# Feature attention as a ring of eight PSUM banks, a transposed output product in the ternary layer, norms computed further ahead, and splits placed behind the negated maxima

## The reference

```python
# L0x, L1x: 16 heads of 16; products are made from three bf16 parts of each fp32 operand
attn = softmax(einsum('bhqd,bhkd->bhqk', q, k) / sqrt(16)); out = (attn @ v) @ wo.T + bo

# L1f: block_quant rounds to 3 mantissa bits, one exponent for each 32 features
h = gelu(block_quant(x) @ block_quant(w_fc).T + b_fc)          # 256 -> 1024
return block_quant(h) @ block_quant(w_proj).T + b_proj         # 1024 -> 256

# L2x: softmax over the 16 FEATURES of a head, for q and for k
q = softmax(_heads(x @ Wq.T + bq), axis=-1)
k = softmax(_heads(y @ Wk.T + bk), axis=-1);  v = _heads(y @ Wv.T + bv)
D_inv = 1.0 / sum(q * sum(k, axis=-2), axis=-1)
out = q + (q @ einsum('bhnd,bhne->bhde', k, v)) * D_inv
return out @ Wp.T + bp

# L2f: weights rounded to -1, 0, 1 by their mean magnitude
h = relu(x @ quantize(W1).T + b1);  return h @ quantize(W2).T + b2
```

## Time and profile before

| what | us |
|---|---|
| median of 3 runs (lowest to highest) | 4759.7 (4759.58 to 4760.19) |
| the profiled execution: its time | 4758.25 |
| the profiled execution: its span | 4756.4 |
| PE busy | 4330.5 (91%) |
| PE weight load busy | 2408.4 (51%) |
| DVE busy | 3124.3 (66%) |
| ACT busy | 2460.3 (52%) |
| POOL busy | 899.1 (19%) |
| softmax_attentions | 0 to 1812 |
| quantised_ffn | 1812 to 2026 |
| feature_attention | 2026 to 2282 |
| ternary_ffn | 2282 to 2588 |
| the two stages after them | 2588 to 4756.4 |

### The profile page before, as it was taken

How to read it: one execution, slowest core, us unless ns; L and a number is a source line. 1 busy time by engine, 2 the same in 40 slices (tenths; PEclk the granted TensorE clock), 3 DMA queues, 4 the chain that set the end, 5 groups by cost and what they waited for, 6 DMA issues and landing times. The chain is left out here.

```text
span 4756.4 us, 67654 instructions
## 1 busy us (share of the span) xinstructions
PE 4330.5 (91%) x23938; PEld 2408.4 (51%) x23938; DVE 3124.3 (66%) x7497; ACT 2460.3 (52%) x5534; POOL 899.1 (19%) x583
## 2 busy tenths in 40 slices
PE   5999999999999995677576999999999998999998
PEld 2333334443333333455354666666666666555555
DVE  5777777777777775778665667767666766334333
ACT  3666666666666665511232677677767676111111
POOL 2322443533223203511243000000000000000000
PEclk8999999999999997889687999999999999999999
DMA  6445345343444420010200011101101101000001
GB/s 146 76 71 82 65 58 89 54 67 67 67 79 73 72 41 22 1 36 13 90 0 16 27 32 31 30 30 30 35 26 30 35 26 41 33 0 0 0 0 36
DMA packets 182204, 205.16 MB, mean 43 GB/s; under 512 B 43704, under 2 KB 164408, under 8 KB 180256
## 3 DMA queue, kind: packets, MB, share of 16 engines
q1 hardware_dynamic: 181920, 201.45, 21.4%
HBM read 140.64 MB, written 60.78 MB: 42 GB/s over the span
## 5 line engine op out<-in xcount | busy, mean ns | idle before, releaser
L461 DVE TENSOR_REDUCE L0x_maxes<-L0x_ps_max 128x1 f32<-128x512 f32 x1536 | 986.1, 684 | 275.7 <-PE L0x_ps_max L726 271.9
L642 ACT ACTIVATE L0x_probs<-L0x_ps_sc 128x1024 f32<-128x1024 f32 x768 | 778.5, 1026 | 413.6 <-PE L0x_ps_sc L715 407.9
L726 PE MATMUL L0x_ps_max<-L0x_kstack,L0x_qstack 96*128 96x512 bf16 x1536 | 593.9, 387 | 20.6 <-DVE L0x_maxes L461 12.4
L2431 ACT ACTIVATE L3x_pexp<-L3x_ps,L3x_nmax 128x77 f32<-128x77 f32 (+2 forms) x1536 | 600.3, 432 | 0.0
L715 PE MATMUL L0x_ps_sc<-L0x_qstack,L0x_kstack 104*128 104x512 bf16 x1536 | 523.3, 382 | 8.9 <-ACT L0x_probs L642 5.9
L2313 DVE TENSOR_REDUCE L3x_nmax<-L3x_ps 128x2 f32<-128x154 f32 (+2 forms) x768 | 346.2, 506 | 240.3 <-PE L3x_ps L2544 237.9
L737 PE MATMUL L0x_ps_out<-L0x_probs,L0x_vpad 128*32 128x512 f32 x3072 | 411.7, 608 | 9.1 <-ACT L0x_heads_raw L650 8.6
L2439 ACT COPY L3x_pT<-L3x_ps 128x512 f32<-128x512 f32 x512 | 275.0, 593 | 226.6 <-PE L3x_ps L2552 226.2
L1952 ACT ACTIVATE L3f_act_g<-L3f_ps_gu 128x512 f32<-128x512 f32 x128 | 76.4, 597 | 565.2 <-PE L3f_ps_gu L1997 565.2
L726 PEld LDWEIGHTS L0x_ps_max<-L0x_kstack,L0x_qstack 96*128 96x128 bf16 x1536 | 149.0, 97 | 424.8 <-DVE L0x_maxes L461 320.8
L2329 DVE TENSOR_SCALAR L3x_pexp<-L3x_pexp,L3x_rsum 128x77 f32<-128x77 f32 (+2 forms) x1536 | 357.7, 306 | 6.8
(11 more groups left out here) (356 smaller groups left out, 6993.7 us busy)
## 6 DMA issues: line engine op xcount, KB each, us to landing
L0x_kstack<-parts_scratch SPq DMA_DIRECT2D x144, 256.0 KB, 8.9
L0x_qstack<-parts_scratch SPq DMA_DIRECT2D x144, 256.0 KB, 13.6
parts_scratch<-L0x_kparts SPq DMA_DIRECT2D x24, 768.0 KB, 3.6
parts_scratch<-L0x_qparts SPq DMA_DIRECT2D x24, 768.0 KB, 4.1
rel_scratch<-L3x_rel_e SPq DMA_DIRECT2D x32, 408.0 KB, 2.4
L3x_rel_d<-prob_scratch SPq DMA_DIRECT2D x32, 408.0 KB, 3.1
L0x_kv_in<-in_ctxT SPq DMA_DIRECT2D x16, 512.0 KB, 5.2
L3x_rel_t<-rel_scratch SPq DMA_DIRECT2D x32, 154.0 KB, 2.4
```

What stands on the lines that cost most here:

```text
L461: V.tensor_reduce(maxes[:, t, head:head + 1], ps_max[:, unit % 2, :], AX.X, ALU.max).then_inc(max_taken, 1)
L642: nc.scalar.activation(probs[:, n % 4], ps_sc[:, 2 * (n % 2):2 * (n % 2) + 2, :], ACT.Exp, scale=HD ** -0.5).then_inc(probs_ready, 1)
L726: nc.tensor.matmul(ps_max[:, unit % 2, :], qstack[q.parity][0:ROWS, head, t * P:(t + 1) * P], kstack[q.parity][0:ROWS, head, :], start=Tru ...
L2431: i = nc.scalar.activation(pexp[:, n % 4, e, a:b], ps[:, SB + 2 * (n % 2) + e, a:b], ACT.Exp, bias=nmax[:, n % 4, s, e:e + 1], accum_out=s ...
```

## The change

There are four parts.

1. *softmax_attentions*: GpSimd waits for `negmax_ready` of the running item before the first half of a key split, and for that of the next item's first group before the first half of a query split (cross layers).
2. *quantised_ffn*: `moments`, `deviation` and `normalised` run two sequences ahead, behind unit 2; x of the next sequence is raised, rounded and turned behind unit 0 (unit 1 before); ScalarE's `summed` goes ahead of taking x. The bias is held as 128x10 columns, split by five small VectorE operations, written to DRAM and read back as three rows.
3. *feature_attention*: unrolled rounds r = -2 to 7 on one ring of eight PSUM banks, of which each unit of `ROUND_UNITS` takes the next two or four. The norm moves to ScalarE and runs three sequences ahead; keys, queries, `vx` and `kv_in` are doubled. Keys are not divided: the reciprocals of their sums scale the values instead (`scaled_values`). Queries are not divided either: the attended product has 144 columns, with denominators and query sums in the last 16, and GpSimd's `softmax_of_queries` makes the softmax beside it. The values' bias goes through `wo` into the output's bias once.
4. *ternary_ffn*: unrolled. The output product is transposed (`ps_yT`, weights stationary, 48 matmuls of 512 columns a sequence), taken by ScalarE with b2, turned back (`output_turned`) and added in halves. Hidden blocks run three ahead. The hidden split is VectorE's alone, ScalarE makes the norm two sequences ahead, and weights have a semaphore each.

```diff
 # softmax_attentions, gpsimd
+                    if ahead.later and after_k == 0 and q.there:
+                        pool.wait_ge(negmax_ready, q.count(4, 4))
+                    if ahead.later and after_q == 1 and ahead.cross:
+                        pool.wait_ge(negmax_ready, q.plus(1).count(4, 1))
...
 # quantised_ffn
-            order += [of_hidden(u)] + [of_x(u // TILES + 1)] * (u % TILES == 1 and u // TILES < SEQS - 1)
+            order += [of_hidden(u)] + [of_x(u // TILES + 1)] * (u % TILES == 0 and u // TILES < SEQS - 1)
...
                 if t == 0 and seq < SEQS - 1:
-                    deviation(seq + 1)
-                if t == 1 and seq < SEQS - 1:
                     rounded(of_x(seq + 1))
+                if t == 2 and seq < SEQS - 2:
+                    deviation(seq + 2)
...
+            def bias_split():
+                dve.wait_ge(bias_in, 16)
+                V.tensor_copy(bsplit[:, 0], bias[:]).then_inc(bias_step, 1)
+                dve.wait_ge(bias_step, 1)
+                V.tensor_tensor(bias[:], bias[:], bsplit[:, 0], ALU.subtract).then_inc(bias_step, 1)
...
+                summed(u)
                 if t == 0 and seq < SEQS - 1:
-                    normalised(seq + 1)
-                summed(u)
-                if t == 1 and seq < SEQS - 1:
                     taken(of_x(seq + 1))
+                if t == 2 and seq < SEQS - 2:
+                    normalised(seq + 2)
...
+ROUND_UNITS = (("eT", 0, 2), ("kv", 0, 2), ("q", 1, 2), ("o", 0, 4), ("xnT", 2, 2), ("k", 2, 2), ("hT", 0, 2),
+               ("v", 2, 2), ("y", 0, 2))
...
 # feature_attention, gpsimd
+            def softmax_of_queries(seq):
+                pool.wait_ge(o_rec, seq + 1)
+                if seq:
+                    pool.wait_ge(htok_ready, seq)
+                rest = orec[:, :, H8:].unsqueeze(3).broadcast_to([P, TILES * C, H8, HD])
+                nc.gpsimd.tensor_tensor(soft[:].rearrange("p t (c h e) -> p (t c) h e", c=C, e=HD),
+                                        query[:, seq % 2].rearrange("p t (c h e) -> p (t c) h e", c=C, e=HD), rest,
+                                        ALU.mult).then_inc(soft_ready, 1)
...
+                if there(r):
+                    softmax_of_queries(r)
+                    bias(r)
+                if there(r + 3):
+                    deviation(r + 3)
...
 # feature_attention, vector
+            def key_totals(seq):
+                dve.wait_ge(k_exp, seq + 1)
+                V.tensor_reduce(ktotal[:], heads(key[:, seq % 2]), AX.X, ALU.add).then_inc(k_total, 1)
+                dve.wait_ge(k_total, seq + 1)
+                V.reciprocal(krec[:], ktotal[:]).then_inc(k_rec, 1)
...
+            def attended(seq):
+                dve.wait_ge(in_bank["o"], seq + 1)
+                o = wide("o", seq)
+                V.reciprocal(orec[:], o[:, :, P:WIDE]).then_inc(o_rec, 1)
+                dve.wait_ge(o_rec, seq + 1)
+                V.tensor_tensor(htok[:].rearrange("p t (c h e) -> p (t c) h e", c=C, e=HD),
+                                o[:, :, 0:P].rearrange("p a (h e) -> p a h e", e=HD),
+                                orec[:, :, 0:H8].unsqueeze(3).broadcast_to([P, TILES * C, H8, HD]),
+                                ALU.mult).then_inc(taken["o"], 1)
+
+            def whole(seq):
+                dve.wait_ge(taken["o"], seq + 1)
+                dve.wait_ge(soft_ready, seq + 1)
+                V.tensor_tensor(htok[:], htok[:], soft[:], ALU.add).then_inc(htok_ready, 1)
...
+            for r in range(-2, SEQS + 1):
+                if there(r - 1):
+                    summed(r - 1)
+                if there(r + 1):
+                    key_totals(r + 1)
+                if there(r):
+                    blocks_kept(r)
+                if there(r + 1):
+                    scaled_values(r + 1)
+                    take_queries(r + 1)
+                if there(r):
+                    attended(r)
+                    whole(r)
+                if there(r + 1):
+                    shift_queries(r + 1)
+                if there(r + 2):
+                    take_keys(r + 2)
+                if there(r + 3):
+                    moments(r + 3)
...
 # ternary_ffn, vector
+            def hidden_split(g):
+                slot = g % 4
+                dve.wait_ge(h_high, 2 * g + 2)
+                if g >= 2:
+                    dve.wait_ge(h_low, g - 1)
+                V.tensor_tensor(hrest[:, g % 2], hf[:, g % 3], hparts[:, slot, 0], ALU.subtract).then_inc(h_rest, 1)
+                dve.wait_ge(h_rest, g + 1)
+                V.tensor_copy(hparts[:, slot, 1], hrest[:, g % 2]).then_inc(h_mid, 1)
+                dve.wait_ge(h_mid, g + 1)
+                V.tensor_tensor(hparts[:, slot, 2], hrest[:, g % 2], hparts[:, slot, 1], ALU.subtract).then_inc(h_low, 1)
...
+                hidden_split(g)
+                if f == 1 and seq < SEQS - 1:
+                    tokens_rest(C * seq + C)
+                    tokens_rest(C * seq + C + 1)
+                if f == 2 and seq:
+                    summed(2 * seq - 2)
+                    summed(2 * seq - 1)
+                if f == 3 and seq < SEQS - 1:
+                    tokens_low(C * seq + C)
+                    tokens_low(C * seq + C + 1)
+                if f == 4 and seq < SEQS - 2:
+                    moments(seq + 2)
...
 # ternary_ffn, scalar: order behind rectified(g)
+                if f == 2 and seq:
+                    output(seq - 1)
+                if f == 3 and seq < SEQS - 1:
+                    tokens_high(C * seq + C)
+                    tokens_high(C * seq + C + 1)
+                if f == 5 and seq < SEQS - 1:
+                    tokens_mid(C * seq + C)
+                    tokens_mid(C * seq + C + 1)
+                if f == 7 and seq < SEQS - 2:
+                    normalised(seq + 2)
...
 # ternary_ffn, tensor
+            def projected(g):
+                seq, f = g // KH, g % KH
+                if f == 0 and seq:
+                    pe.wait_ge(yT_ready, C * seq)
+                pe.wait_ge(h_low, g + 1)
+                for c in range(C):
+                    for part in range(3):
+                        i = nc.tensor.matmul(ps_yT[:, c, :], w2q[:, f, c * P:(c + 1) * P], hparts[:, g % 4, part, :],
+                                             start=(f == 0 and part == 0), stop=(f == KH - 1 and part == 2))
+                i.then_inc(h_used, 1)
```

More of the change, by code:

```diff
@@ L1316, in feature_attention @@
+        q_top, q_shifted, q_exp = ph.sem("q_top"), ph.sem("q_shifted"), ph.sem("q_exp")
+        o_rec, soft_ready, htok_ready = ph.sem("o_rec"), ph.sem("soft_ready"), ph.sem("htok_ready")
         W = T[name]
         NW = 7
-        block = ph.stack.enter_context(nc.Block())
+        bank, before, last, at = {}, {}, {}, 2
+        for r in range(-2, SEQS):
+            for what, ahead, size in ROUND_UNITS:
+                if 0 <= r + ahead < SEQS:
+                    mine = [(at + k) % 8 for k in range(size)]
+                    bank[what, r + ahead] = mine[0]
+                    before[what, r + ahead] = sorted({last[b] for b in mine if b in last})
+                    last.update({b: (what, r + ahead) for b in mine})
+                at += size
@@ new lines, in _ @@
+            normalised(0)
+            for r in range(-2, SEQS):
+                if there(r + 1):
+                    exponentials(r + 1, key, k_shifted, k_exp)
+                if there(r):
+                    turned("eT", r, qT)
+                if there(r + 2):
+                    turned("xnT", r + 2, xnT)
+                if there(r):
+                    turned("hT", r, hT)
+                if there(r + 1):
+                    exponentials(r + 1, query, q_shifted, q_exp)
+                if there(r + 2):
+                    take_values(r + 2)
+                if there(r + 3):
+                    normalised(r + 3)
@@ L1517, in body, with product @@
-            def body(seq, more):
-                pe.wait_ge(v_ready, seq + 1)
-                pe.wait_ge(k_soft, seq + 1)
+                        i = nc.tensor.transpose(out[:, c, t * P:(t + 1) * P], src[:, t, c * P:(c + 1) * P], ident[:])
+                i.then_inc(in_bank[what], 1)
+            def product(what, seq, rows, weights):
+                out = wide(what, seq)
+                for t in range(TILES):
+                    for c in range(C):
+                        i = nc.tensor.matmul(out[:, t], rows[:, c, t * P:(t + 1) * P], weights[c],
+                                             start=(c == 0), stop=(c == C - 1))
+                i.then_inc(in_bank[what], 1)
@@ new lines, in _ @@
+            moments(1)
+            magnitude(1, w2, w2_in)
+            ternary(1, w2, w2q)
+            for g in range(STEPS_F):
+                seq, f = g // KH, g % KH
[10 more added lines that the diff above has]
+                if f == 4 and seq < SEQS - 2:
+                    moments(seq + 2)
@@ new lines, in output @@
+            def output(seq):
```

(12 more changed lines are left out.)

822 lines of the change are left out of this document (445 added, 377 removed).

## The result

The changed kernel takes 4616.5 us, the median of 4 runs (4613.49 to 4620.15), against 4759.64 us for the kernel before: a ratio of 0.9704, 95% interval 0.9689 to 0.9718. The forecast was 4623 us with a range of 4582 to 4672. The profiled execution has a span of 4615.2 us against 4756.4.

What follows compares the result with a forecast made beforehand. Three stages (quantised_ffn, feature_attention, ternary_ffn) were taken as bound by a chain round the engines once per sequence. Savings of 18 + 27 + 12 + 80 = 137 us from 4758.25 gave 4621 profiled, 4623 median; range 4582 to 4672.

Steps and rivals of the forecast that it cites:

- softmax_attentions, -18: softmax_attentions: the two new GpSimd waits regain 0.8 us for each of 23 TensorE waits, between 0 and 24.9 in all.
- rival (d): softmax_attentions: the waits do not do what they say, the 18 us are gone, 4641 us; chance inside the forecast's 0.64.
- quantised_ffn, -27: quantised_ffn: period falls from 23.15 to 20.0 us, saving 22 us, plus 5 at the opening; bounds -10 and -33.
- the opening: quantised_ffn: VectorE's first hidden activation comes at 1837.5 instead of 1842.67, saving 5 us.
- The three thin slacks: quantised_ffn: units 2, 3 and the next 0 have slacks of 1.9, 0.2 and 0.3 us; period taken as 20.0.
- feature_attention, -12: feature_attention: round falls from 28.8 to 25.6 us, saving 19 us, less about 7 at filling and last rounds; bounds +15, -37.
- The hold: feature_attention: GpSimd's bias holds SBUF so whole() starts behind it; TensorE idles 2.5 us a round, plus 1.0 for its clock.
- TensorE's own 22.1 us: feature_attention: TensorE's work in a new round, four products, two smaller products and three turnings, sums to 22.1 us.
- ternary_ffn, -80: ternary_ffn: TensorE bounds it, period falls from 34.3 to 24.5 us, end at 2506.5 instead of 2586.9; bounds -50 and -92.
- (a): Queues' order binds more: late steps cost 3 us a sequence in feature_attention and ternary_ffn, quantised_ffn's slacks go; 4665 us; chance 0.18.
- (b): feature_attention: whole() is not held behind the bias, 18 us more saved, 4605 us, or 4593 with ternary_ffn's -92; chance 0.14.
- (c): feature_attention and ternary_ffn: TensorE is granted the lower clock level, 315 us more, 4938 us; chance 0.03.

Runs made afterwards that it cites:

- e10: The changed kernel without the key split's wait anywhere, the query split's wait kept: 4611.5 us, ratio 0.969.
- e1: The changed kernel with both new GpSimd waits of softmax_attentions taken out: 4625.7 us, ratio 0.9731.
- e5: The changed kernel itself, run again beside the kernels with one stage put back: 4612.1 us, ratio 0.970.
- e8: The changed kernel with ternary_ffn as before the change: 4704.6 us, ratio 0.9894.
- e3: The changed kernel with the key split's wait left out only while a mixture item's gates are worked out: 4600.9 us, ratio 0.968.
- e6: The changed kernel with quantised_ffn and its bias array as before the change: 4641.5 us, ratio 0.9762.
- e7: The changed kernel with feature_attention as before the change: 4629.2 us, ratio 0.9735.
- e4: The changed kernel with GpSimd's bias addition of feature_attention moved behind the deviation, one sequence ahead: 4601.4 us, ratio 0.9683.
- e11: The changed kernel with ternary_ffn's hidden blocks two ahead instead of three: 4663.8 us, ratio 0.9803.
- e12: The changed kernel with the first subtraction of ternary_ffn's hidden split (the remainder) back on GpSimd: 4639.6 us, ratio 0.9751.
- e2: The changed kernel with the key split's wait kept only where the keys are of a cross layer: 4613.0 us, ratio 0.9704.
- e9: The changed kernel with the edits of e3 and e4 together: 4583.2 us, ratio 0.9633.

## Why the prediction was right, step by step

**What bounds the kernel.** Right: the three stages were bound by chains round the engines, and each got shorter when the chain did.

**softmax_attentions, -18: the term that failed.** The cross layers gave a little more than I charged, 0.92 us a round against 0.8 (69.45 for 70.37), by the query split's wait (e10). The step that failed is that in the mixture layer the key split would move by a few us into a gap of POOL. It was a gap of POOL, but not of VectorE: its gate operations stand there, and I looked at the moved engine's queue only. Mixture rounds without gates gained 3.7 us each (70.95 against 74.7), five with them lost 4.3 each (78.5 against 74.1). The loss is not the same in every execution: with the same code some of these rounds took 75.9 us, and the mixture layer 649.8 to 657.4 us in eight profiles. In the result's profile the cross layers gained 13.4 us and the mixture lost 8.7: net 5 (also e1, e5 to e8) instead of 18, and rival (d) in all but name. e3 shows what the waits are worth once that is avoided: its stage is 23.8 us shorter than before. The charge per wait was rough too: of the 24.9 us, 8.8 were in the mixture, three waits of 2.4 us and five of 0.32.

**quantised_ffn, -27: right** (28.1; 29.4 by e6). Period 19.73 for 20.0, opening 4.0 us for 5. The terms named for the opening (1820, four turns of 3.53, 1.8 of moments) add up to 1835.9 and not to 1837.5; with that, the forecast would have been 29. The three thin slacks cost little: 19.73 against the 19.4 us of five turns and moments alone. How much of the gain is the norm's lead and how much x's new place, no run separates.

**feature_attention, -12: right in mechanism, off in size** (19.2; 17.1 by e7). The hold came in all 8 rounds, TensorE waited 2.5 to 3.0 us in the five between the first and the last two for a forecast of 2.5, and whole() took 3.27 us for "3.5". The clock cost 1.2 us in every second round, 0.6 a round, for a forecast of 1.0. The mis-sized term is TensorE's own 22.1 us: it measured 20.3 to 20.5 (the sum of start-to-start intervals, 4 x 3.456 + 1.86 + 1.96 + 3 x 0.87, and e4's 21.40 less the 0.93 us wait). I had added durations of groups, and in these rows the next group starts before the end of the one before: products are 3.456 us apart and not 3.72, turnings 0.87 and not 1.04. Which of the stage's other edits gave how much, no run separates. The filling and the last rounds lost 6 x 4.75 - 19.2 = 9.3 us for the 7 charged. Of the hold, the Trainium skill (SBUF — State Buffer, the section on who interferes with whom) says that order of issue decides and that the pair is held for the whole instruction. The trace agrees: the sum took 3.27 us in each round where the bias had started first, in the changed kernel and in e4, and in the mixture 128x4 elements waited until GpSimd's operation was over. The row on which the forecast rested is another case: the scaling of the earlier trace rows has one tensor input, and it was held as well (the first of the four takes 2.45 us, the others 0.40 each).

**ternary_ffn, -80: right in mechanism, off in size** (92.9; 92.6 by e8). The period is 23.37 us for 24.5: 0.2159 us a matmul for 0.219 (0.3 us), the same overlap at the turnings (0.4), and a wait of 0.73 for 1.4. Seven periods gave 77 us where I had put 69, so opening and tail gave 16 where I had put 11; what of that is the clock, no run separates. e11 and e12 show the two things on which it rests: three blocks ahead (50 us) and GpSimd's queue kept off the split (28 us). What the turned product is worth by itself no run shows. The Trainium skill (TensorE: Matmul & The Clock Gate, the section on 56 ns) gives 215.7 ns from start to start for 512 columns at 2.4 GHz; the trace agrees, and that would have been the better term than mine from a group's duration.

**Rivals.** (a), late steps at 3 us a sequence: only the 0.73 us wait. (b), no hold: contradicted by every round. (c), the lower level: the granted clock is 0.88, 0.88 and 0.94 in the three stages, from 0.82, 0.88 and 0.81. That the sum came within 4.2 us of the span is luck: the 13.3 us missing in the first term were made up by 7.2 and 12.9 in the last two. The total alone would hide that.

## What to carry to other kernels

Before moving a GpSimd operation, look at what VectorE does at its new place and not only at GpSimd's gap: an operation on 4 elements a partition waits out the whole instruction. Where both engines have work on SBUF in the same chain, put what has slack (a bias, a norm) where VectorE idles, reduces, or reads one of its two inputs from PSUM. One input alone is not enough: the negation, the scaling and the CAST have one tensor input and were held here. Price a TensorE stream by start-to-start intervals, and a depth of lookahead by the longest run of other work between two of its steps and not by the engines' busy shares.

## What the runs showed of the hardware

- VectorE operations on 128x4 elements took 1.78 and 1.84 us beside a GpSimd subtraction and 0.16 us otherwise; the cost of a hold is GpSimd's remaining time, whatever the size.
- Held were additions and products of two SBUF tiles, and also operations with one tensor input: the negation on 128x16 elements (0.18 us alone, up to 2.11 in the kernel before and 1.20 in the changed one), a scaling of 128x256 (2.45 for 0.40) and a CAST of 128x512 (1.36 for 0.42). Not held beside a GpSimd operation were reductions (L465, 0.69 us, 455 times in the changed kernel) and additions of a PSUM and an SBUF tile (L481, 0.69 us, 13 times).
- The length of an idle did not alone decide TensorE's level: behind 2.54 us the turning of htok took 1.09 us in most rounds, but 1.97 us once in each of eight profiles (e1, e2, e3, e5, e6, e8, e10, e11). Behind 2.97 us it took 1.7 to 2.0 in the changed kernel, and 1.09 in e4 and e9, where the idles before it had been 0.93 us at most. With no idle over 0.93 us (e4) it never fell in the steady rounds.
- The same code took 1802.3 to 1811.6 us for one stage and 2167.9 to 2172.1 us for another between executions, with different granted clocks in them. In the last two stages, 2172.0 to 2172.1 us went with a granted clock of 0.72 in the first 60 us, and 2167.9 to 2168.6 with 0.80. A difference of 5 us between two single profiles of this kernel is not a finding.
